# Inverting the slot table of a mixture-of-experts layer with bf16 one-hots, and reordering what stands around it

## The reference, cut to what matters

```python
h = tok(x)                                  # image tokens at three scales, fused; (4, 256, 192)
h = concat([h, txt], axis=1)                # (4, 384, 192)
h = h + mamba(layernorm(h))                 # state-space block, 16 states, sequence 384, own norm at its end
xf = layernorm(h).reshape(1536, 192)
logits = xf @ Wr.T                          # 8 experts
topk_vals, topk_idx = top_k(logits, 2)
weights = softmax(topk_vals)
out_e = gelu(xf @ Wi[e].T + bi[e]) @ Wo[e].T + bo[e]      # F = 768
h = h + sum_k weights[k] * out_e[topk_idx[k]]
```

## Time and profile before

| | us |
|---|---|
| median of three runs | 445.19 |
| the profiled execution | 445.39 |
| its span, first to last instruction | 443.6 |
| PE busy | 373.6 (84%) |
| PEld busy | 280.8 (63%) |
| DVE busy | 274.4 (62%) |
| POOL busy | 233.7 (53%) |
| ACT busy | 197.9 (45%) |

### The profile page before, as it was taken

The page is one execution under the profiler, slowest core; times in us unless marked ns, Lnnn a source line. Parts: engine busy times, 40 slices in busy tenths (PEclk is TensorE's granted clock), DMA queues, the critical chain, the costliest instruction groups (busy, mean ns, idle before and its releaser), DMA issues.

```text
span 443.6 us, 6744 instructions
## 1 busy us (share of the span) xinstructions
PE 373.6 (84%) x2265; PEld 280.8 (63%) x2265; DVE 274.4 (62%) x470; ACT 197.9 (45%) x502; POOL 233.7 (53%) x171
## 2 busy tenths in 40 slices
PE   5889897999748958698777795899999999999970
PEld 4445654554424625354445574799999999999970
DVE  4525479898999999979992569244434343443400
ACT  1456576576824575535650220044443544444440
POOL 6877733567456737656462005334655556565431
PEclk9999997899969989989699877699999999999996
DMA  6310014453537756857374530422232322323224
GB/s 186 65 12 4 7 33 135 118 120 104 161 79 224 210 170 176 254 169 230 126 218 176 201 108 0 131 44 48 52 55 48 50 53 45 59 41 53 39 28 115
DMA packets 36038, 46.01 MB, mean 104 GB/s; under 512 B 8813, under 2 KB 25022, under 8 KB 35438
## 3 DMA queue, kind: packets, MB, share of 16 engines
q1 hardware_dynamic: 28686, 38.00, 28.8%
q0 software_dynamic: 7328, 7.71, 11.1%
HBM read 39.69 MB, written 7.18 MB: 106 GB/s over the span
## 4 chain that ended last, share of the span: by engine, by line
PE 40%; DVE 20%; issue 14%; POOL 12%; DMA 4%; SPq 4%; ACT 2%; POOLq 0%; DVEq 0%; ACTq 0%
PE ps L1073 15%; PE ps L1056 9%; DVE w_all L1585 7%; POOL w_all L577 6%; PE ps L1062 6%; DVE ps L1577 4%; POOL w_all L627 4%; PE ps L1032 2%; SPq L502 2%; DVE y_cm L1531 2%; DVE y_cm L1503 2%; PE ps L1046 2%; PE ps L887 1%; DVE stats L1440 1%; DMA b_wide_sb<-bc_dram 1%
## 5 line engine op out<-in xcount | busy, mean ns | idle before, releaser
L627 POOL TENSOR_TENSOR w_all<-w_all 128x768 f32<-128x768 f32 x48 | 80.5, 1681 | 75.2 <-DVE w_all L1585 32.2
L660 POOL DMA_INDIRECT sum_dram<-u_cm,tok_row x31 | 50.6, 1632 | 60.1 <-ACT u_cm L1406 50.3
L887 PE MATMUL ps<-w_all,cst 128*128 128x512 f32 x96 | 57.3, 681 | 21.8 <-POOL w_all L627 21.6
L1585 DVE TENSOR_TENSOR_SCAN w_all<-decay,ps 128x780 f32<-128x780 f32 x40 | 71.1, 1779 | 1.5 <-POOL w_all L627 0.2
L577 POOL DMA_INDIRECT w_all<-in_pix,gidx x42 | 45.7, 1089 | 14.7 <-issue 12.5
L1391 ACT ACTIVATE u_cm<-ps,x_cm 128x128 f32<-128x128 f32 x96 | 26.6, 377 | 54.5 <-PE ps L1062 54.5
L645 POOL DMA_INDIRECT dt_cm<-x_dram,tok_in x31 | 31.2, 1007 | 19.3 <-DVE gate_s L1750 10.1
L1577 DVE TENSOR_TENSOR ps<-dtu_cm,ps 128x768 f32<-128x768 f32 x40 | 37.9, 948 | 4.6 <-ACT ps L1306 2.8
L823 PE MATMUL ps<-cst 128*128 128x256 f32 x128 | 35.1, 429 | 5.3 <-DMA cst<-in_cst 5.3
L887 PEld LDWEIGHTS ps<-w_all,cst 128*128 128x128 f32 x96 | 17.2, 205 | 33.5 <-POOL w_all L627 29.1
L1763 DVE COPY x_cm<-w_all 128x1154 f32 x16 | 12.2, 762 | 40.2 <-PE ps L1073 40.2
(11 more groups left out here) (229 smaller groups left out, 696.4 us busy)
## 6 DMA issues: line engine op xcount, KB each, us to landing
w_all<-bc_dram SPq DMA_DIRECT2D x48, 256.0 KB, 3.4
w_all<-bc_dram SPq DMA_DIRECT2D x96, 64.0 KB, 3.5
w_all<-in_w_all SPq DMA_DIRECT2D x16, 289.0 KB, 4.1
w_all<-in_w_all SPq DMA_DIRECT2D x4, 1156.0 KB, 6.2
b_wide_sb<-bc_dram SPq DMA_DIRECT2D x8, 256.0 KB, 3.7
x_dram<-x_cm SPq DMA_DIRECT2D x3, 384.0 KB, 3.1
sum_dram<-h_tok SPq DMA_DIRECT2D x3, 384.0 KB, 3.5
out<-sum_dram SPq DMA_DIRECT2D x4, 288.0 KB, 3.8
```

The costliest lines, as they stand in the source:

```text
L627: nc.gpsimd.tensor_tensor(segments(hcs[at % 2]), inner(states[at % 2]), segments(c_sb[at % RING]), ALU.mult).then_inc(hc_rdy, 1)
L660: pool.indirect_dma_start(sum_dram, bass.IndirectOffsetOnAxis(ap=tok_row[:, i:i + 1].bitcast(U32), axis=0), y_out[:, i % 2, :], None, comp ...
L887: nc.tensor.matmul(sums[:, 0:4 * P], ident, hcs[at % 2][:, 0:4 * P], start=False, stop=at % S == S - 1, skip_group_check=True)
L1585: v.tensor_tensor_scan(states[p], fade, drive, 0.0, ALU.mult, ALU.add).then_inc(scanned, 1)
```

## The change

- **bf16 one-hots.** `cnt`, the running counts, the slot's two parts, `at_lo` and `what` are bf16 and hold small whole numbers, which bf16 keeps exactly. Compare tables (1 MB, at the end of `cst`) are loaded into `u_cm` in scan step 39. `at_lo` is laid out [slot, pair], so that one instruction covers 12 pairs; TensorE reads it and `what` at a step of 24 elements. The token number goes as two parts (`what` 0 and 1), and `what` 2 tells the choice. POOL has no part in it.
- **Tiles by rounding.** The slot's tile comes from adding and taking away 1.5 * 2**30, whose last place is 128.
- **Gates travel with the rows.** Both gates (the first, and the second less the first) are two more columns of `xf` and `x_dram`; each tile's gate is made by one more VectorE operation (`gates`), and ScalarE and the fetch wait for it.
- **Bias rows behind the inversion,** and their additions behind the first tile's up weights.
- **Last C product** by VectorE instead of POOL.
- **Loads.** Weight pieces in three of four scan steps from 16, 20 of them (with the last expert's); `send_rows` a step later behind the broadcast; router buffers elsewhere.
- `WARM`: "slots" 4 to 9, "bias rows" 2 new, "first tile" 6 to 3.

```diff
+                if at == 2 * S + 7:
+                    sp.wait_ge(summed, 2 * S + 1)
+                    sp.dma_start(u_cm[:, 0:N_TAB // 2], d["cst"][:, N_CST:N_CST + N_TAB // 2]).then_inc(ld_tab, 16)
+                if at >= S and at % 4 != 3 and loaded < len(loads):
+                    load_expert(*loads[loaded], PIECES)
+                    loaded += 1
...
+            sp.wait_ge(route, ROUTE_GATES)
+            for j in range(NJ):
+                send_gates(j)
...
-            for at in range(STEPS):
+            for at in range(STEPS - 1):
...
-            pool.wait_ge(route, ROUTE_HI)
-            for k in range(TOPK):
-                nc.gpsimd.tensor_tensor(what[:, k, :, 0, :], at_hi[:, k, :, :],
...
+                    pool.wait_ge(gate_rdy, i + 1)
...
+            pe.wait_ge(ld_tab, 16)
             pe.wait_ge(route, ROUTE_CNT)
+            rank = ps[:, 6, 0:E * (NT + 1)]
+            nc.tensor.matmul(rank, all_ones, run, start=True, stop=False, skip_group_check=True)
+            nc.tensor.matmul(rank.rearrange("p (e t) -> p e t", e=E)[:, :, 0:NT], below, cnt[:, :, 1:NT + 1],
+                             start=False, stop=True, skip_group_check=True).then_inc(cnt_ps, 1)
+            keep_warm(WARM["slots"], 7)
+
+            for k in (1, 0):
+                pe.wait_ge(route, ROUTE_LO[1 - k])
+                for t in range(NT * k, NT * k + NT):
+                    mm = nc.tensor.matmul(ps[:, 7, 0:(2 + k) * MT].rearrange("p (w m) -> p w m", m=MT), at_lo[:, :, t],
+                                          what[:, 0:2 + k, :, t], start=(t == NT), stop=(t == NT - 1),
+                                          skip_group_check=True)
+            mm.then_inc(tok_ps, 1)
+
+            pe.wait_ge(route, ROUTE_E8)
             for j in range(NJ):
...
             mm.then_inc(gt_ps, 1)
             pe.wait_ge(gt_rdy, 1)
+            keep_warm(WARM["bias rows"], 6)
...
+            pe.wait_ge(h_final, 1)
             x_transposed(0, 0)
+            pe.wait_ge(h_final, NB)
+            up(0, 0)
             x_transposed(1, 1)
-            up(0, 0)
+            pe.wait_ge(h_final, NB + 2)
...
+            def last_product():
+                dve.wait_ge(scanned, STEPS)
+                dve.wait_ge(c_ready[(STEPS - 1) % RING], 48 * ((STEPS - 1) // RING + 1))
+                dve.wait_ge(summed, STEPS - 2)
+                v.tensor_tensor(segments(hcs[(STEPS - 1) % 2]), inner(states[(STEPS - 1) % 2]),
+                                segments(c_sb[(STEPS - 1) % RING]), ALU.mult).then_inc(last_hc, 1)
...
+            rt(v.tensor_scalar(raised[:, :], total, HALF, TO_TILE, ALU.add, ALU.add))
+            rt(v.tensor_scalar(whole[:, :], raised[:, :], -TO_TILE, None, ALU.add))
+            rt(v.tensor_tensor_scan(ends[:, 1:1 + E], ones_e[:, :], whole[:, :], -HALF, ALU.mult, ALU.add))
+            rt(v.tensor_tensor(pos[:, :, :], rank[:, :, 0:NT].rearrange("p e t -> p t e"),
...
+            rt(v.tensor_scalar(slot_hi, slot_f, TO_TILE, -TO_TILE, ALU.add, ALU.add))
+            rt(v.tensor_tensor(slot_lo, slot_f, slot_hi, ALU.subtract))
+            dve.wait_ge(ld_tab, 16)
+            rt(v.tensor_tensor(what[:, 2, :, :], slot_hi.rearrange("p (o t) -> p o t", o=1)
+                               .to_broadcast([P, MT, TOPK * NT]), iota_hi, ALU.is_equal))
+            v.tensor_scalar(what[:, 0, :, :], what[:, 2, :, :], cst[:, C_P:C_P + 1], None, ALU.mult).then_inc(route, 1)
+            v.tensor_tensor(what[:, 1, :, :], what[:, 2, :, :], tile_no.to_broadcast([P, MT, TOPK * NT]), ALU.mult)\
+                .then_inc(route, 1)
...
+                v.tensor_tensor(at_lo[:, :, half], slot_lo[:, half].rearrange("p (o t) -> p o t", o=1)
+                                .to_broadcast([P, P, NT]), iota_lo[:, :, half], ALU.is_equal).then_inc(route, 1)
...
             e = up_weights(0, 0)
+            for b in range(NB):
+                dve.wait_ge(bo_ps, b + 1)
+                v.tensor_tensor(h_tok[:, 0:2, b, :], h_tok[:, 0:2, b, :],
+                                ps[:, b, :].rearrange("p (j c) -> p j c", j=2)[:, :, 0:C], ALU.add).then_inc(h_final, 1)
...
             tokens(0, 0)
+            gates(0, 0)
             down_weights(0, 0, e)
...
+            def gates(i, q):
+                v.scalar_tensor_tensor(gate_q[:, q:q + 1], x_in[:, q, CW + 1:XW], found[:, 2, bass.ds(i, 1)],
+                                       x_in[:, q, CW:CW + 1], ALU.mult, ALU.add).then_inc(gate_rdy, 1)
```

More of the change, by code:

```diff
@@ L168, in build @@
         rstd = sb("rstd", [P, 3, NT])
-        gate = sb("gate", [P, TOPK, NT])
+        gate_1 = sb("gate_1", [P, NT])
+        gate_q = sb("gate_q", [P, NX])
         gtmp = sb("gtmp", [P, 2, NT])
-        tiles = sb("tiles", [P, E])
-        ends = sb("ends", [P, E])
-        first = sb("first", [P, E])
+        raised = sb("raised", [P, E])
+        whole = sb("whole", [P, E])
+        ends = sb("ends", [P, 1 + E])
         logit = sb("logit", [P, NT, E])
@@ L383, in build @@
         WARM = {"input weights": 10, "coarse levels": 2, "fine patches": 4, "patches": 7, "normed rows": 7, "convolution": 2,
-                "first step": 12, "router's rows": 14, "counts": 6, "slots": 4, "first tile": 6}
+                "first step": 12, "router's rows": 14, "counts": 6, "slots": 9, "bias rows": 2,
+                "first tile": 3}
         STEPS = NJ * S
@@ L535, in _ @@
             broadcast_b(5)
-            piece = 0
+            loaded = 0
             for at in range(RING, STEPS):
@@ L548, in _ @@
                     sp.wait_ge(xt_ready, 6)
[L549 to L554, removed]
+                    sp.wait_ge(dtu_rdy, 3)
+                if at == 2 * S + 7:
[4 more added lines that the diff above has]
+                    loaded += 1
+            assert loaded == len(loads)
             sp.wait_ge(summed, STEPS)
@@ L1025, in _ @@
                                  start=True, stop=True).then_inc(bo_ps, 1)
-            keep_warm(WARM["slots"], 7)
-            for k in range(TOPK):
-                pe.wait_ge(route, ROUTE_LO + k)
-                pe.wait_ge(whats, k + 1)
-                for t in range(NT):
-                    mm = nc.tensor.matmul(ps[:, 7, 0:2 * MT], at_lo[k][:, t, :],
-                                          what[:, k, t, :, :].rearrange("p w m -> p (w m)"),
-                                          start=(k == 0 and t == 0), stop=(k == TOPK - 1 and t == NT - 1))
-            mm.then_inc(tok_ps, 1)
             keep_warm(WARM["first tile"], 6)
-            pe.wait_ge(h_final, 1)
             def x_transposed(i, q):
@@ L1723, in _ @@
-            rt(ins)
-            assert at_r == ROUTE_HI, at_r
-            for k in range(TOPK):
-                rt(v.tensor_tensor(at_lo[k], dig[:, 1, k, :, :].to_broadcast([P, NT, P]), iota_p, ALU.is_equal))
-            t31 = cst[0:P, C_IOTA:C_IOTA + MT].rearrange("p (m o) -> p m o", o=1)[0:1].to_broadcast([1, MT, E])
-            rt(v.tensor_tensor(tcmp[:, :, :], ends[0:1, :].rearrange("p (o e) -> p o e", o=1).to_broadcast([1, MT, E]),
+            rt(v.reciprocal(gate_0, gtmp[:, 1, :]))
```

289 lines of the change are left out of this document (148 added, 141 removed).

## The result

The changed kernel takes 439.75 us (median of four, 438.79 to 441.08) where the kernel before took 445.06 beside it: a ratio of 0.9873, with a 95% interval from 0.9839 to 0.9907. It is 5.3 us faster; 12.3 were forecast, and 439.75 lies above the range's upper end of 438.0. The profiled execution took 440.68, its span 438.9.

The account below looks back on a forecast made before the run. Bound: VectorE in the scan, TensorE in the expert loop, a chain of waits between, where nearly the whole change is. Sum: 1.65 - 0.15 + 0.35 + 13.25 - 0.8 - 2.0 = 12.3, median 432.9; 80% range 430 to 438.

Parts of the forecast that it names:

- End of the scan, 1.65: Scan's end: C row sent ahead of the x_dram rows starts product 46 earlier, 1.65 us gained; product 47's move worth nothing.
- rival of the starved scan: Scan: added weight pieces and the table delay C rows; at 1.0 us a piece 20 us lost, 452.9; chance 0.05.
- Router tail and counts: Before the one-hots: memsets cost 0.15 us, bf16 count instructions save about 0.35; VectorE resumes at 260.3, not 262.15.
- VectorE's passes: Counts to one-hots: bf16 passes at the lower end, 0.54 us for 744 elements and 0.95 for 1536.
- rival of slow passes: One-hot passes: VectorE does bf16 comparisons at the f32 rate, 2.9 us worse, 435.8; chance 0.10.
- The inversion: Slot-table inversion on TensorE: two batches of 12 bf16 pairs, 0.11 us each, 1.3 a batch; VectorE later by 0.2.
- rival of strided operands: Inversion: TensorE's 48-byte step makes the second batch end 2.5 us later, 435.4; chance 0.17.
- What is late next, first tile at 274.2: Fetch to first tile: TensorE's part ends about 273, VectorE sets the first tile at 274.2, not 288.50; 14.3 us gained.
- The second tile, 2.0: Second tile's transpose behind the first's up matmuls: first up to first down 6.9 us, not 4.88; 2.0 lost.
- The loop at nothing: Expert loop: one more VectorE gate operation per tile and waits on POOL and ACT cost nothing.
- The sum: All terms together: 12.3 us gained, 433.1 profiled and 432.9 median; chance 0.52 of 430.8 to 434.6.
- The clock rival: Inversion: granted clock rises only behind the fillers, batches at half rate, about 3.2 us late, 436.1; chance 0.12.

Follow-up runs that it names:

- e12: The kernel before with only the x_dram rows sent one step later, behind the C row's broadcast: 442.29 us, ratio 0.9948.
- e11: The changed kernel with the last C product on POOL again, as before the change: 438.57 us, ratio 0.9848.
- e2: The changed kernel without the fillers at the bias rows and the first tile: 434.2 us, ratio 0.9750.
- e1: The changed kernel run again with no edit: 437.91 us, ratio 0.9816 to the kernel before.
- e4: The changed kernel with bias rows in front of the inversion, their additions in VectorE's gaps, three slots and four first-tile fillers: 433.14 us, ratio 0.9712.
- e9: Against e10, eight fillers behind the inversion in place of four: 431.36 us, ratio 0.9676 to the kernel before.
- e8: The changed kernel with at_lo laid out [pair, slot], so TensorE reads its weights without a step: 477.05 us against 482.61 for the kernel before, ratio 0.9880.
- e3: The changed kernel with one f32 filler behind every fourth matmul of the inversion: 436.51 us, ratio 0.9827.
- e5: The changed kernel with the second tile's transposes ahead of the first tile's up matmuls: 473.27 us against 482.61 for the kernel before, ratio 0.9814.
- e7: The changed kernel with the edits of e4 and e5 together: 468.1 us against 482.61 for the kernel before, ratio 0.9716.
- e10: The same kernel as e7 on another chip, with 4 fillers behind the inversion: 431.98 us against 445.32 for the kernel before, ratio 0.9687.

## Why the prediction was wrong, point by point

- *End of the scan, 1.65.* Right: 1.64 in the changed kernel, and e12 shows that the order alone brings product 46 to its scan and 1.25 of it. The product's move is worth nothing (e11). That scan 47 ended 0.9 us earlier than before I don't put down to the change, though no run separates it: VectorE's wait in step 36 was 0.48 us in place of 2.17, with the clock at 1.00 there and not 0.50, and the scan's end moved between 230.9 (e12) and 235.6 us (e2) in the profiles of e1 to e4 and e9 to e12. The scan as a whole took 151.1 us in place of 151.5, so the rival of the starved scan is out.
- *Router tail and counts.* Right within 0.9, all of it from the item above.
- *VectorE's passes.* Right at the lower end (0.55 and 0.91). The rival of slow passes is out here, and e8 shows when it comes true.
- *The inversion.* A mis-sized term: 0.15 a pair, 3.6 us for 24, where I had 2.6. The step of 48 bytes is not the reason (e8: 0.144 without it), nor the clock (e1). So TensorE and not VectorE was the later of the two: VectorE waited 1.20 us for it. That the first fetch still left on time is luck, since VectorE's one-hots began 0.9 earlier. The rival of strided operands is false at its size: the step costs 0.15 us in all and not 2.5.
- *What is late next, first tile at 274.2.* This is the step that failed. It had TensorE's part end "about 273", all at full-clock prices, because, as the rival on the clock said against itself, "TensorE is now idle nowhere over 2 us between counts and loop". The clock fell at 266, in the inversion, with TensorE busy, and the bias rows, their five fillers and the transposes then kept TensorE from 268.75 to 277.42: 8.7 us, where the same work takes 4.7 in e3 at the full clock. VectorE, which I held to set the tile, waited 2.15 us for it. The first up was 9.4 us behind the fetch, with 5.55 forecast. It took both to lose this: with the clock up it is 5.3 (e3), and at the low clock without the fillers it is 5.3 as well (e2).
- *The second tile, 2.0.* The place was right and the size was not. I counted 6.9 us from first up to first down; they were 9.2 in the changed kernel, of which up matmuls at half clock are 2.1, and 9.3 in e3, where the first up ran at full clock but the second tile waited and then ran at the low clock. With the transposes first it is 5.5 (e5), and with the clock up besides 4.9 (e9).
- *The loop at nothing.* Right: 136.89 against 136.88.
- *Scatter chain.* Not in my list. TensorE ends 6.2 us earlier than before, the last scatter only 5.2 and the span 4.7: the third last landed in 4.61 us, and each of the last two waits for the one before it. In e1 it is 4.62 too, in e3 a scatter near the end took 3.52. What makes it slow is open.

The sum, against the 433.1 of the profiled execution: 3.8 for the first up, 2.3 from there to the first down product, 1.5 behind the loop make the 7.6 by which it missed. The clock rival, at 0.12, suspected the right thing for the wrong reason. It feared that the low stretch from 250.6 would end late, priced only the inversion's batches by it (3.2 us), and looked for idle time as the cause. The clock rose in time (259.1) and fell later, with TensorE busy, and the price was paid by all that TensorE had on the path until the next rise, 17 us later. That its 436.1 lies nearer to the result than the sum does is no merit of its mechanism. (The forecast read the low stretches of before as 250.6 to 260 and from 272 on the earlier trace rows; in finer windows they run from 250.6 to 260.9 and from 271.1 to 284.8. Nothing in the sum hangs on it.)

What is still open is what makes the clock fall: it did so between 3.4 us (e4) and 24 us (e3) behind its rise. In seven of the ten profiles with nothing f32 inside the inversion (all but e4, e7 and e9) it fell in the inversion or within 1.3 us of its end, in e10 behind 6 us in which TensorE was busy throughout; in the two with f32 fillers inside it did not. This speaks for the small bf16 matmuls as a cause, and no run shows it. They are not the only one: in e12, which has none of them there, it fell at 262.5 among the f32 fillers, and in e4 and e7 it fell 5.4 and 4.6 us behind the inversion, where TensorE had just waited 2.2 us for the first fetch; in e9 more fillers stood in that wait and it did not fall. From one profile a kernel I can't say more.

## What to carry to other kernels

Price TensorE's work behind a stage that is driven by waits at both clock levels, and let the low one decide what may stand on the path: the bias rows with their fillers took 4.7 us at the one level and 8.7 at the other. Fillers that don't hold the clock are only more work. When a stage is cut in half, the work that used to hide under it (here the bias rows) must find another cover: in front of the inversion the first up came 3.9 us behind the fetch (e4), behind it 5.3 at the full clock (e3) or without fillers (e2), and 9 at the low one with them. And keep the transposes of the second item in front of the first item's products.

## What the runs showed of the hardware

The granted clock went to the 1.2 GHz level while TensorE was busy 5.94 of 6.60 us, and stayed there for 17 us of 93% busy time. In e1 it fell 1.3 us behind the same 24 matmuls. A weight load of 128 columns and a matmul of 62 or 93, in bf16, take 0.15 us together, in e1 all at the full clock and in the changed kernel 1.6 of 3.6 us at the low one. VectorE's bf16 comparison takes 0.91 us for 1536 elements with an innermost step of one in every operand, and 1.71 with a broadcast innermost. In e3 and e4 VectorE's copy of the second tile's up weights came 1.12 and 1.03 us behind its predecessor, in the changed kernel, e1 and e2 0.32; why was not tried.
